# Top-k threshold search: three of four masks on VectorE, the fourth counted on ScalarE by summed signs

## The reference

```python
adj = emb_s * emb_t * softmax(attention_weights) / sqrt(n)
adj[:, diag, diag] = -inf
_, idx = top_k(adj.reshape(g, n * n), 5120)
out = zeros((g, n * n)).at[rows, idx].set(1.0)
```

## Time and profile before

| what | number |
|---|---|
| median of 3 runs | 4073.15 us (4071.14 to 4074.32) |
| the profiled execution, first to last instruction (span) | 4078.2 us |
| busy over the span | PE 91%, DVE 67%, ACT 51%, POOL 12% |
| high half of the search, in the trace | 31.1 to 124.8 us |
| low half of the search | 133.9 to 207.6 us |

### The profile page before, as it was taken

The page is one execution under the profiler, slowest core; times in us unless marked ns, Lnnn a source line. Parts: engine busy times, 40 slices in busy tenths (PEclk is TensorE's granted clock), DMA queues, the critical chain, the costliest instruction groups (busy, mean ns, idle before and its releaser), DMA issues. The chain is left out here.

```text
span 4078.2 us, 177223 instructions
## 1 busy us (share of the span) xinstructions
PE 3719.3 (91%) x70140; PEld 2792.5 (68%) x70140; DVE 2749.4 (67%) x10621; ACT 2082.2 (51%) x7371; POOL 478.1 (12%) x411
## 2 busy tenths in 40 slices
PE   2458888888999999999999998999999999999999
PEld 2425465554699999999999996565456546644664
DVE  8878788786677777777777776576367537653763
ACT  4028678677755555555555553453245315532542
POOL 2006366364000000000000000001000100010001
PEclk9979999998755555555555556999999999999999
DMA  2023132231000000000000003211221141023102
GB/s 93 1 89 94 48 110 87 60 106 56 4 6 6 6 6 6 6 6 6 6 6 6 6 6 137 83 41 42 109 90 34 42 158 52 23 83 124 44 14 93
DMA packets 113888, 203.31 MB, mean 50 GB/s; under 512 B 44076, under 2 KB 76844, under 8 KB 111416
## 3 DMA queue, kind: packets, MB, share of 16 engines
q1 hardware_dynamic: 113720, 201.00, 14.8%
HBM read 160.05 MB, written 32.52 MB: 47 GB/s over the span
## 5 line engine op out<-in xcount | busy, mean ns | idle before, releaser
L1521 PE MATMUL gru_sum_n<-gru_state_parts,w_hh_hi 128*128 128x8 f16 x8192 | 499.6, 174 | 0.0
L1511 PE MATMUL gru_sum_n<-gru_state_parts,w_hh_lo 128*128 128x4 f16 x8192 | 488.9, 168 | 0.0
L1511 PEld LDWEIGHTS gru_sum_n<-gru_state_parts,w_hh_lo 128*128 128x128 f16 x8192 | 376.5, 104 | 0.0
L1521 PEld LDWEIGHTS gru_sum_n<-gru_state_parts,w_hh_hi 128*128 128x128 f16 x8192 | 376.5, 104 | 0.0
L653 ACT ACTIVATE dit_prob<-dit_bank,dit_head_nbias 128x512 f32<-128x512 f32 x256 | 175.9, 687 | 351.0 <-DVE dit_head_nbias L671 350.6
L1654 DVE TENSOR_TENSOR_SCAN gru_n_in<-gru_reset_gate,gru_sum_n 128x32 f32<-128x32 f32 x1024 | 225.4, 220 | 54.7
L1511 PE MATMUL gru_sum_rb<-gru_state_parts,w_hh_lo 128*128 128x4 f16 x4096 | 261.3, 168 | 0.0
L1521 PE MATMUL gru_sum_za<-gru_state_parts,w_hh_hi 128*128 128x8 f16 x4096 | 254.1, 169 | 0.0
L1521 PE MATMUL gru_sum_ra<-gru_state_parts,w_hh_hi 128*128 128x8 f16 x4096 | 254.1, 168 | 0.0
L1521 PE MATMUL gru_sum_zb<-gru_state_parts,w_hh_hi 128*128 128x8 f16 x4096 | 254.1, 168 | 0.0
L1511 PE MATMUL gru_sum_zb<-gru_state_parts,w_hh_lo 128*128 128x4 f16 x4096 | 252.1, 166 | 0.0
(11 more groups left out here) (335 smaller groups left out, 12378.5 us busy)
## 6 DMA issues: line engine op xcount, KB each, us to landing
dit_w_qk<-w_qk_parts SPq DMA_DIRECT2D x64, 512.0 KB, 3.6
room<-w_parts SPq DMA_DIRECT2D x8, 4096.0 KB, 12.8
room<-w_v_parts SPq DMA_DIRECT2D x5, 4096.0 KB, 12.2
room<-w_out_parts SPq DMA_DIRECT2D x4, 4096.0 KB, 14.8
small_given_w<-in_L_cond_qkv_w SPq DMA_DIRECT2D x48, 256.0 KB, 3.1
w_qk_parts<-small_parts_w SPq DMA_DIRECT2D x32, 256.0 KB, 2.1
small_given_w<-in_L_cond_ffn_w SPq DMA_DIRECT2D x32, 256.0 KB, 3.7
w_parts<-small_parts_w SPq DMA_DIRECT2D x32, 256.0 KB, 2.4
```

The source lines that it names most:

```text
L1511: mm = pe.matmul(columns[:, j, 0], w_hh[1][:, k, c:c + P], parts[:, par, 0, k, :, LAST], start=opens, stop=False, skip_group_check=True)
L1521: mm = pe.matmul(columns[:, j], w_hh[0][:, k, c:c + P], parts[:, par, :, k, :, LAST], start=opens, stop=False, skip_group_check=True)
```

## The change

- The mask of batch 3 (`LAST_B`) is not made by VectorE, nor counted by the 16 matmuls. ScalarE computes the sign of (candidate minus key) over the 2048 elements with the sum along the row as accumulator output (`weigh_last`, L260 after), and a second small instruction turns the sum into a count (2048/2 minus half of the sum, L264) in the last column of `part16`. The candidates stand half a unit lower, so that no sign is zero. TensorE's `sum_up` of pair 1 waits for this too (`balance_copied`), and the sign of the next count waits for the last decision of pair 1 (`cand_ready[1]`).
- VectorE makes three masks a pass, and `copy_part(0, k)` stands ahead of the last mask instead of behind it.
- ScalarE's other work goes between the counts: the four `lo` keys behind counts 2 to 5 of the high half, then one instruction of the weight split behind each count. The split has eight pieces of 768 columns and four of 512, in four buffers.

The diff, cut to its core:

```diff
-    SLOTS, WIDE = 2, 1536
+    SLOTS, WIDE = 4, 768
...
+            def weigh_last(half, i):
+                n = half * (BITS + 1) + i
+                if i:
+                    act.wait_ge(cand_ready[1], half * BITS + i + 2)
+                elif half:
+                    act.wait_ge(lo_keyed, 1)
+                else:
+                    act.wait_ge(search_begun, 1)
+                    act.wait_ge(hi_made, B)
+                act.activation(mask[:, LAST_B, :], (hi, lo)[half][:, LAST_B, :], ACT.Sign,
+                               scale=turned_sign[:, LAST_B:B] if half == 0 else -1.0, bias=cand[:, LAST_B:B],
+                               accum_out=balance[:]).then_inc(balance_ready, 1)
+                act.wait_ge(balance_ready, n + 1)
+                act.activation(part16[:, LAST_B:B], balance[:], ACT.Identity, scale=-0.5, bias=half_row[:])\
+                   .then_inc(balance_copied, 1)
...
+            LO_FROM = 2
+            for i in range(BITS + 1):
+                weigh_last(0, i)
+                if LO_FROM <= i < LO_FROM + B:
+                    low_half(i - LO_FROM)
+                elif i >= LO_FROM + B:
+                    split_beside(i - (LO_FROM + B))
+            for i in range(BITS + 1):
+                weigh_last(1, i)
+                if i:
+                    split_beside(i + (BITS - LO_FROM - B))
...
             def sum_up(g, i):
                 pe.wait_ge(part_copied[g], i + 1)
+                if g == 1:
+                    pe.wait_ge(balance_copied, i + 1)
...
                     counts(0, 1, i)
+                    sum_up(0, i)
                     counts(1, 0, i)
-                    sum_up(0, i)
-                    counts(1, 1, i)
...
                     dve.wait_ge(ge_ready[g], decided + 1)
-                    dve.tensor_scalar(cand[:, p], ge[:, p], -1.0, float(1 << 14) + 1.0, ALU.mult, ALU.add)\
+                    dve.tensor_scalar(cand[:, p], ge[:, p], -1.0, float(1 << 14) + 0.5, ALU.mult, ALU.add)\
...
                     let_in(0, 1)
                     decide(1, k - 1)
+                    copy_part(0, k)
                     let_in(1, 0)
-                    copy_part(0, k)
-                    let_in(1, 1)
                     decide(0, k)
...
                     step(ins)
+                    dve.sem_inc(lo_keyed, 1)
```

More of the change, by code:

```diff
@@ L90, in sync, with high, scale @@
             sp.dma_start(self.slot(j), src).then_inc(self.loaded[j % self.SLOTS], 16)
[L92 to L96, removed]
+    def high(self, act, j):
+        _, hi, _, scale = self.pieces[j]
+        act.wait_ge(self.loaded[j % self.SLOTS], 16 * (j // self.SLOTS + 1))
+        act.activation(hi, self.slot(j), ACT.Copy, scale=scale)
+    def scale(self, act, j):
+        act.activation(self.slot(j), self.slot(j), ACT.Copy, scale=self.pieces[j][3]).then_inc(self.scaled, 1)
     def pool(self, pool):
@@ L109, in topk_phase @@
     E = T * D // P
+    BITS, LAST_B = 16, B - 1
+    LET_IN = ((0, 0), (0, 1), (1, 0))
     with ExitStack() as ctx:
@@ L239, in _, with low_half @@
                     exponentials(b + 2)
-            split.scalar(act)
-            for b in range(B):
+            def weigh_last(half, i):
[13 more added lines that the diff above has]
+                   .then_inc(balance_copied, 1)
+            def low_half(b):
                 act.wait_ge(sign_found[b // 2], 1)
@@ L244, in _, with split_beside @@
                                bias=lo_shift[:, b:b + 1]).then_inc(lo_made, 1)
+            def split_beside(n):
+                if n < 2 * len(split.pieces):
+                    (split.high, split.scale)[n % 2](act, n // 2)
+            LO_FROM = 2
[9 more added lines that the diff above has]
+                    split_beside(i + (BITS - LO_FROM - B))
             act.wait_ge(emb_ready, 1)
@@ L307, in _ @@
                 sum_up(1, base + BITS - 1)
-                for g in range(2):
-                    for j in range(2):
-                        counts(g, j, base + BITS)
+                for g, j in LET_IN:
+                    counts(g, j, base + BITS)
                 for g in range(2):
@@ L352, in _ @@
             dve.memset(want[:], float(TOPK))
-            dve.memset(cand[:], 0.0)
+            dve.memset(cand[:], -0.5)
             dve.memset(sign[:], 1.0)
+            dve.memset(turned_sign[:], -1.0)
+            dve.memset(half_row[:], float(E // 2)).then_inc(search_begun, 1)
             dve.memset(zeros[:], 0.0)
@@ L430, in _ @@
                 opening = find_sign if half == 0 else lambda g: decide(g, 0)
-                for b in range(B):
+                for b in range(LAST_B):
                     if half == 0:
@@ L462, in _ @@
                 decide(1, BITS - 1)
[L464 to L467, removed]
+                for g, j in LET_IN:
+                    let_in(g, j)
+                step(dve.scalar_tensor_tensor(out=found[:, half, :], in0=cand[:], scalar=0.5, in1=sign[:],
                                               op0=ALU.subtract, op1=ALU.mult))
@@ L474, in _ @@
                 if half == 0:
-                    dve.memset(cand[:], 32768.0)
+                    dve.wait_ge(balance_ready, BITS + 1)
+                    dve.memset(cand[:], 32767.5)
                     dve.wait_ge(lo_made, B)
```

18 lines of the change are left out of this document (12 added, 6 removed).

## The result

The median fell from 4073.74 to 4049.74 us (four runs each, 4071.14 to 4074.61 and 4048.43 to 4054.21), a ratio of 0.9941 [0.9927, 0.9955]. The profiled execution of after has a span of 4047.2 us and a time of 4049.04. A second trace of before has a span of 4074.7 and a time of 4076.53, so a time stands 1.8 us above its span, and both traced executions of before ran longer than their median (the first, of 4078.2, by some 6 us).

A forecast was written before the change was run, and what follows sets the result against it. VectorE's own instructions were taken to bound the search: 23.4 - 4.4 - 1.7 - 1.3 - 0.3 + 0.3 + 0.9 = 16.9 us, say 17, so 4073.15 - 17 = 4056 us; range 4046 to 4066.

The forecast's parts named there:

- VectorE bounds the search: Search: VectorE's own instructions set the pass; one mask fewer in each of 34 counts gains 23.4 us.
- The copy's wait: Search passes: VectorE waits 0.16 us at pair 0's copy, 4.4 us back over 29 passes; POOL's subtractions hide 0.9.
- The sign: ScalarE's search loop: sign with accumulator read takes 2.18 us, loop 3.36, leaving some 0.6 of slack.
- C: Rival, ScalarE in the search: table loads of 1.28 us before and behind each sign, 47 us more, 4120; chance 0.03.
- `lo` keys and count 15: Search, places where ScalarE is late: 1.7 us back at the low keys, 1.3 at the two halves' last decisions.
- POOL: Weight split beside the search: POOL works 19.4 us, VectorE loses 14.2, 0.43 covered per subtraction; a gain of 0.3.
- the 4.9 us: Weight split: if a running mask holds POOL off too, nothing is covered and the result is 4.9 us worse, about 4061.
- The step that fell short: Phases behind the search: they start earlier by the search's gain, with the same instructions; about 17 us in all.
- The span against the median: Whole kernel: the runs' median stands 5 us under the profiled span of 4078.2, so 4061 becomes 4056.
- A: Rival, search: ScalarE becomes the bound with a sign of 3.03 us; gain falls to 6.8, 4066; chance 0.08.
- B: Rival, search: slack used better, no waits at copies, keys or late decisions, POOL half covered; gain 28, 4045; chance 0.05.
- D: Rival, behind the search: a later phase waits for something that does not move; no change, about 4072; chance 0.04.

The follow-up runs named there:

- scalar_free: After, but ScalarE's sign reads constants and its count goes to a spare column, so pair 1's sum does not wait for it: 4046.94 us.
- after_no_pool: After without POOL's twelve subtractions in the weight split (lower weight parts set to zero): 4037.10 us, ratio to before 0.9906.
- scalar_plus_1024: After with one more ScalarE copy of 1024 columns ahead of each of the 34 signs: 4063.11 us, ratio to before 0.9965.
- after_pe_pad: After with 160 more one-column matmuls on TensorE ahead of the GRU's loop: 4055.71 us, ratio to before 0.9951.
- the 512 columns: After with one more ScalarE copy of 512 columns ahead of each of the 34 signs: 4053.85 us, ratio to before 0.9945.

## Why the prediction was right, and where it was not

- **VectorE bounds the search.** Right: the end of the search moved by 17.0 to 17.3 us for a sum of 16.9, two passes take 7.94 and 7.68 (7.9 and 7.8 forecast), and scalar_free shows that only 3 us hang on ScalarE.
- **The copy's wait.** 0.22 to 0.23 for 0.16; it stands in 13 passes, with 0.16 in one more and 0.06 to 0.13 in four of the first, 3.5 us in all. That is the 3.5 of the sum (4.4 less 0.9), but by luck: the wait is longer than said, and POOL's work hides it wholly in 11 passes where the sum has it hidden by half in 12.
- **The sign.** 2.18 with its read, as taken from the `lo` key. No table load stands in the search (the trace of after has one at 2.3 us and the next at 265), so C falls. The Trainium skill ("ScalarE: Activation LUTs", section "Table sets: the hidden batching unit") left this open; the trace settles it for sign with Identity, Copy and exponential.
- **`lo` keys and count 15.** Three ge beside the keys wait 0.43, 0.24 and 0.61: 1.3 us for 1.7. At count 15 the waits are 0.76 and 0.73, 1.5 us for 1.3. One place the sum has otherwise: at count 0 VectorE's wait of 1.28 us for batch 3's key is gone, and the sign's decision of pair 1 waits 1.33 for ScalarE's count in its place. The two rows, of before and of after, and the end of the high half in after:

```profile
34.99 0.81 DVE L387 TENSOR_SCALAR edge_mask<-edge_key_hi,edge_sign,edge_cand 128x2048 f16<-128x2048 int16 x1 [1.28 <-ACT edge_key_hi L232]
```

```profile
37.71 0.16 DVE L458 TENSOR_TENSOR edge_ge<-edge_total,edge_want 128x2 f32<-128x2 f32 x1 [1.33 <-PE edge_total L330]
...
102.10 0.16 DVE L438 CAST edge_part<-edge_part 128x1 f16<-128x1 f32 x1 [0.21 <-PE edge_part L321]
...
103.16 0.16 DVE L447 TENSOR_TENSOR edge_ge<-edge_total,edge_want 128x2 f32<-128x2 f32 x1 [0.76 <-PE edge_total L330]
...
103.69 3.56 DVE L429 TENSOR_SCALAR edge_mask<-edge_key_hi,edge_sign,edge_cand 128x2048 f16<-128x2048 int16 x3
```

- **POOL.** Its groups after, beside the earlier trace rows:

```profile
L103 POOL TENSOR_TENSOR small_qkv_lo<-edge_split_stage,small_qkv_hi 128x768 f16<-128x768 f32 x8 | 13.8, 1724 | 99.1 <-ACT edge_split_stage L98 99.1
L103 POOL TENSOR_TENSOR small_out_lo<-edge_split_stage,small_out_hi 128x512 f16<-128x512 f32 x4 | 6.0, 1501 | 28.0 <-ACT edge_split_stage L98 28.0
```

It works 19.8 us (19.4 forecast). Twelve VectorE instructions are stretched: six low to 1.60, four to 1.12, one cand to 1.25 and the three masks at 103.69 to 3.56 (2.26 in after_no_pool); with their usual times off they lose 14.2 (14.2 forecast). (19.8 - 14.2) / 12 = 0.47 us of each are not lost (0.43 forecast). Where that lies, POOL's rows show:

```profile
85.22 1.76 POOL L103 TENSOR_TENSOR small_qkv_lo<-edge_split_stage,small_qkv_hi 128x768 f16<-128x768 f32 x1 [7.45 <-ACT edge_split_stage L98]
...
152.65 1.50 POOL L103 TENSOR_TENSOR small_out_lo<-edge_split_stage,small_out_hi 128x512 f16<-128x512 f32 x1 [6.99 <-ACT edge_split_stage L98]
```

The first ends at 86.98, and the `low` that began at 85.40 ends at 87.00: VectorE goes on when POOL is done. That agrees with the exclusive lock of the Trainium skill ("SBUF — State Buffer", section "Who interferes with whom"). Both subtractions begin while a mask is still running. The second begins 0.41 earlier than the `low` that it stretches to 1.12 (153.06). In scalar_plus_1024 all twelve begin with no mask running, and take 1.15 for 512 columns and 1.64 for 768; of before's four of 512, one began 0.64 before the `low` that it stretched, beside a mask, and took 1.73 where the others took 1.15 to 1.18 (ns: smallest, median, largest; scalar_plus_1024, then before):

```profile
L103 POOL TENSOR_TENSOR small_out_lo<-edge_split_stage,small_out_hi x4: 1151/1152/1152, 161.3 to 189.5; 128x512 f16<-128x512 f32 x4
```

```profile
L101 POOL TENSOR_TENSOR small_out_lo<-edge_split_stage,small_out_hi x4: 1151/1166/1734, 55.6 to 64.3; 128x512 f16<-128x512 f32 x4
```

A head start of 0.18, 0.41 and 0.64 us on the `low`, beside a mask, thus makes the record 0.12, 0.35 and 0.58 longer: nearly all of that time is a wait for the mask, as the rule has it, and not work that a mask covers. POOL's work proper is 8 x 1.64 + 4 x 1.15 = 17.7 us, of which (17.7 - 14.2) / 12 = 0.29 each are not lost. So the term came out right by the same bookkeeping before and after, not by its reason; and the 4.9 us that the prediction worked out from the rule did not come, since the work of which nothing would be covered is less than the 19.4 that it took.
- **The step that fell short** is in the sum: "the next phases start with it: their instructions are the same". They start 17 us earlier, but the GRU then takes 4 to 5 us less, with the same instructions at another place in TensorE's program (after_pe_pad). Of the 5 to 7 us by which the gain of 22 to 24 exceeds the 17, that is the shown part.
- **The span against the median.** The sum used the 5 us between the first trace's span and the median as an offset; that execution was a long one, and a time is 1.8 us above its span. It did no harm, since the forecast is the median less 17.

Of the rivals, A (ScalarE the bound) is refuted by scalar_free and by the 512 columns that a plain pass takes, B by the waits that remain at the copies, C by the missing table load, D by phases that start sooner. The number alone would not have told: 4049.74 lies 6.3 from the forecast and 4.7 from B's 4045; it is the end of the search, at 17 us and not 28, that decides.

## What to carry to other kernels

Where one engine's own instructions set a loop, move one of them to an idle engine and count that engine's whole loop, waits included; the gain is the instruction less the first wait it uncovers, and the places without slack (ends of the loop, odd work in between) pay first. Then look for work that fits into the waits left over: here this was worth another 4.6 us, and writing the loop out 7.0. Compare phases that were not touched, too: here code taken out ahead of a long loop changed what its jump costs.

## What was not expected of the hardware

The step with the jump of TensorE's loop in the GRU is 0.09 us longer than the others with before's program and 0.055 with after's, and 160 matmuls ahead of the loop bring the longer one back (they took 4.21 us themselves, which VectorE's preparation of the loop hid). VectorE's jump in the search costs 0.36 to 0.38 us in the high half (4.15 against 3.79) and 0.45 to 0.51 in the low one, about a tenth of a pass. A subtraction of 512 columns on POOL takes 1.15 us in scalar_plus_1024, where no mask runs as it begins, and 1.50 in all four cases of after, where one does; the mean of 1.30 in before mixes 1.15 to 1.18 with one 1.73.
